# Expert tiles in two phases behind the last attention batch, and the transposed score maxima in another bank

## What is computed

```python
x = x + tanh(g_xattn[0]) * xattn(layernorm(x), ctx, ctx, Wq, bq, Wk, bk, Wv, bv, Wo, bo)
x = x + tanh(g_ffn[0]) * ffn(layernorm(x), norm_scale, w_router, w_up, w_down)

def ffn(x, ...):                       # 8 experts, 352 hidden values, the best 2 of 8 for each token
    xn = rms_norm(x, norm_scale)
    scores = einsum('bsd,ed->bse', xn, w_router)
    _, ids = top_k(scores, 2)
    c = take_along_axis(softmax(scores), ids)
    val, gate = split(einsum('bsd,ehd->bseh', xn, w_up), 2)
    y = einsum('bseh,edh->bsed', val * silu(gate), w_down)
    return sum(take(y, ids) * c) + x
```

## Time and profile before

| what | us |
|---|---|
| median of 3 runs | 489.53 |
| lowest and highest of them | 489.14, 492.61 |
| the profiled execution | 488.46 |
| its span, first to last instruction | 486.7 |
| busy: PE, DVE, ACT, POOL | 395.8, 300.7, 259.8, 249.0 |
| first send, last send of the expert tiles (start) | 308.38, 480.38 |

### The profile page before, as it was taken

One profiled execution on the slowest core, in us unless ns is written; L12 is line 12 of the kernel. 1 busy time (PEld: TensorE's weight loads), 2 busy tenths in 40 slices (PEclk: granted clock), 3 DMA queues, 4 the chain that ended last, 5 costly groups with the idle time before them and its releaser, 6 DMA issues.

```text
span 486.7 us, 13346 instructions
## 1 busy us (share of the span) xinstructions
PE 395.8 (81%) x3788; PEld 269.2 (55%) x3789; DVE 300.7 (62%) x1112; ACT 259.8 (53%) x578; POOL 249.0 (51%) x205
## 2 busy tenths in 40 slices
PE   7578788888979788897987313999999999999960
PEld 3234445464655546455644202777777778777750
DVE  6377678788877887877773430555555555555440
ACT  3232658687676777785757301555455555545520
POOL 4464204136544565635344562456675665667574
PEclk9867899989899998998979555999999999999996
DMA  6331514037377703314011122334353443444230
GB/s 182 105 89 41 143 35 126 22 111 195 87 203 222 185 25 99 92 57 144 26 42 58 55 82 61 65 50 61 52 60 47 57 55 50 55 53 60 21 27 4
DMA packets 57413, 38.99 MB, mean 80 GB/s; under 512 B 8820, under 2 KB 55031, under 8 KB 57367
## 3 DMA queue, kind: packets, MB, share of 16 engines
q1 hardware_dynamic: 42614, 28.24, 22.0%
q0 software_dynamic: 12736, 8.64, 12.8%
q10 hardware_dynamic: 2016, 1.52, 1.2%
HBM read 14.29 MB, written 11.75 MB: 54 GB/s over the span
## 4 chain that ended last, share of the span: by engine, by line
PE 50%; DVE 16%; issue 10%; DMA 9%; ACT 4%; SPq 4%; POOL 3%; POOLq 2%; ACTq 1%; another core or an unknown queue 1%; DVEq 0%
DMA out<-ys,yi 7%; PE bank L1373 6%; PE bank L1351 6%; PE bank L1353 6%; DVE nmx L769 4%; PE bank L1176 4%; PE bank L1363 3%; SPq L237 3%; PE bank L1163 3%; PE bank L1097 2%; PE bank L1193 2%; PE bank L1150 2%; PE bank L1209 2%; ACT pt L542 2%; PE bank L1205 2%
## 5 line engine op out<-in xcount | busy, mean ns | idle before, releaser
L481 POOL DMA_INDIRECT out<-ys,yi x72 | 112.3, 1559 | 74.5 <-issue 37.1
L401 POOL DMA_INDIRECT slots_dram<-xr,slu x64 | 63.8, 997 | 69.3 <-ACT pt L542 47.5
L769 DVE TENSOR_REDUCE nmx<-bank 128x4 f32<-128x512 f32 x128 | 85.7, 676 | 11.9 <-PE bank L1150 11.5
L542 ACT ACTIVATE pt<-bank 128x512 f32<-128x512 f32 x128 | 72.9, 595 | 17.3 <-PE bank L1163 16.5
L1056 DVE TENSOR_TENSOR hh<-sg,bank 128x352 f32<-128x352 f32 x72 | 37.5, 521 | 54.3 <-PE bank L1353 39.3
L1373 PEld LDWEIGHTS bank<-wf_sb,hT 128*128 128x128 f32 (+1 forms) x432 | 56.7, 190 | 23.7 <-issue 19.8
L1373 PE MATMUL bank<-wf_sb,hT 128*128 (+1 forms) x432 | 61.0, 277 | 4.0 <-DVE hT L1066 4.0
L688 ACT ACTIVATE ys<-bank,yc 128x128 f32<-128x128 f32 x72 | 26.4, 367 | 63.7 <-PE bank L1373 33.4
L1351 PE MATMUL bank<-wf_sb,xT 128*128 x144 | 56.0, 471 | 0.0
L1176 PE MATMUL bank<-pt,v 128*9 128x128 f32 x1024 | 50.8, 282 | 6.1 <-ACT pt L542 5.3
L1353 PE MATMUL bank<-wf_sb,xT 128*128 x144 | 55.0, 464 | 0.0
(11 more groups left out here) (163 smaller groups left out, 708.2 us busy)
## 6 DMA issues: line engine op xcount, KB each, us to landing
qs<-parts SPq DMA_DIRECT2D x48, 128.0 KB
ks<-parts SPq DMA_DIRECT2D x42, 128.0 KB
xs<-slots_dram SPq DMA_DIRECT2D x72, 66.0 KB
wf_sb<-in_wup SPq DMA_DIRECT2D x8, 352.0 KB
x_sb<-in_x SPq DMA_DIRECT2D x8, 256.0 KB, 3.3
ctx_sb<-in_ctx_in SPq DMA_DIRECT2D x8, 256.0 KB
out<-x_sb SPq DMA_DIRECT2D x8, 256.0 KB
out<-ys,yi POOLq DMA_INDIRECT x72
```

Of the source, the lines that this page charges most:

```text
L401: nc.gpsimd.indirect_dma_start(out=slots_dram, out_offset=bass.IndirectOffsetOnAxis(ap=slu[:, c % 2, k, kk:kk + 1], axis=0), in_=xr[:, c % ...
L481: nc.gpsimd.indirect_dma_start(out=out.rearrange("b s d -> (b s) d"), out_offset=bass.IndirectOffsetOnAxis(ap=yi[:, r:r + 1], axis=0), in_ ...
L542: nc.scalar.activation(pt[:, 4 * g:4 * g + 4, :], STB[g % 2][:, :].rearrange("p (h s) -> p h s", h=4), ACT.Exp, scale=SCORE_SCALE).then_in ...
L769: nc.vector.tensor_reduce(nmx[:, b % 2, at:at + 4], SB[g % 2][:, :].rearrange("p (h s) -> p h s", h=4), AX.X, ALU.max, negate=True).then_i ...
```

## The change

1. **Two phases.** A first phase of TA = 32 tiles takes only full tiles out of the first NA = 5 chunks. Its table is computed inside the attention loop: counts at b = 26, prefix at b = 29, table at b = 30. The second phase takes the other 40 tiles, again in the order of the experts, from a table made at tiles 14 to 20 of the first phase. The 32 is what is surely there: (2 * 5 * 512 - 8 * 127) // 128, rounded down to a multiple of 8.
2. **No tail of the loop.** The attention loop ends with b = 31. What is left of attention and routing for chunks 6 and 7 is handed out between the tiles of the first phase by `routing(t)` (DVE does the row numbers of chunk 6 at tiles 1 to 3, chunk 7 at 7 to 13, the second table at 15 to 20) on PE, ACT and DVE. POOL does the eight scatters of chunk 6 before sends 4 to 7 and those of chunk 7 before sends 14 to 17, two at a time. SP does the stores of chunks 6 and 7 behind the loads of tiles 7 and 19 and all eight pads behind the load of tile 26. `last_rows` on DVE is gone; ACT makes these rows too. `expert_exp` of chunk 7 now runs at tile 9, after the first silu.
3. **Banks.** The results of `down` have one bank (`Y`, bank 7) in place of two, and `down(t)` waits for `result(t - 1)`. Bank 6 (`TB`) is left for the routing.
4. **Maxima.** `mT_ps` moves from SMALL to the second bank of the scores, SB[1]. The transposition of batch b + 2's maxima, their two parts and their DMAs are done in step b where those of b + 1 were done before: PE transposes behind the last `weighted_values`, DVE splits behind the fourth `maximum`. `scores(b, 1)` gets a wait for `maximum_low(b - 1)`, `transpose_attended(b)` waits for `add_attention(b - 1)` in place of `maximum_low(b + 2)`.
5. **Order on DVE.** `choose_masks` and `choose_sum` come before the third `maximum` of their step, `scales2`, `statistics` and `variance` behind the fourth, `take_positions` and `take_scores` before `add_attention`, `widen` behind it.

The core of the diff (the loops' index of the first body and the code that only changes its place are left out):

```diff
+NA = 5
+TA = (2 * NA * CT - E * 127) // 128 // R * R
+TILE0, TILES = (0, TA), (TA, NT - TA)
+QA = TA // R
-        mT_ps = SMALL[0:NH, 256:384]
+        Y, TB = PR, HB
+        mT_ps = SB[1][0:NH, 0:S]
@@ sync
-                if real(b + 1):
-                    maxima(b + 1)
...
+                if real(b + 2):
+                    maxima(b + 2)
...
+                    if isinstance(q, int):
+                        if t == R - 1:
+                            store(NCH - 2)
+                        if t == 19:
+                            store(NCH - 1)
+                        if t == TA - 6:
+                            pads()
+            sp.wait_ge(d_tab, 1)
+            sp.wait_ge(scattered[0], 16 + 128 * ((NA + 1) // 2))
+            sp.wait_ge(scattered[1], 16 + 128 * (NA // 2))
+            for q in range(QA):
+                body(q)
+            sp.wait_ge(d_tab, 2)
+            sp.wait_ge(padded, 16 * E)
+            sp.wait_ge(scattered[0], 16 + 128 * (NCH // 2))
+            sp.wait_ge(scattered[1], 16 + 128 * (NCH // 2))
@@ gpsimd
-            scatter_rest(NCH - 2, 0)
-            scatter_rest(NCH - 1, 0)
+                    if isinstance(q, int):
+                        if 4 <= t < 4 + CH:
+                            scatter_both(NCH - 2, t - 4)
+                        if 14 <= t < 14 + CH:
+                            scatter_both(NCH - 1, t - 14)
@@ scalar
-            for b in range(B + 2 * CH):
+            for b in range(B):
+            def routing(t):
+                if t == 2:
+                    rows(NCH - 1, (0, 1))
+                if t == 3:
+                    rows(NCH - 1, (2, 3))
+                if t == 5:
+                    rows_transposed(NCH - 1)
+                if t == 7:
+                    base(NCH - 1)
+                if t == 9:
+                    expert_exp(NCH - 1)
@@ vector
+                if u == 0 and there(c - 2):
+                    choose_masks(c - 2)
+                    choose_sum(c - 2)
                 if real(b + 2):
                     maximum(b + 2, 2)
+                if real(b + 2):
+                    maximum(b + 2, 3)
...
+                    maximum_high(b + 2)
+                    maximum_low(b + 2)
...
+                if b == CH * (NA + 1) + 2:
+                    tiles_counted(0)
+                if b == CH * (NA + 2) + 1:
+                    tiles_spread(0)
...
+                if b == CH * (NA + 2) + 1:
+                    tiles_taken(0)
+                if b == CH * (NA + 2) + 2:
+                    tiles_listed(0)
+            def routing(t):
+                c = NCH - 2
+                if t == 1:
+                    scales2(c + 1)
+                    probabilities(c, 0)
+                    place_rows(c)
+                if t == 2:
+                    probabilities(c, 1)
+                    place(c)
+                if t == 3:
+                    probabilities(c, 2)
+                    place_numbers(c)
+                c = NCH - 1
+                if t == 7:
+                    take_scores(c)
+                    choose_values(c)
+                if t == 8:
+                    choose_experts(c)
+                if t == 9:
+                    choose_masks(c)
+                    choose_sum(c)
...
+                if t == 15:
+                    tiles_counted(1)
+                if t == 17:
+                    tiles_spread(1)
+                if t == 18:
+                    tiles_taken(1)
+                if t == 20:
+                    tiles_listed(1)
@@ tensor
+                if g == 1 and b:
+                    pe.wait_ge(d_mT, b)
...
-                if b >= 3:
-                    pe.wait_ge(d_x1, b - 2)
                 nc.tensor.transpose(mT_ps, nmx[:, b % 2, :], ident).then_inc(pe_mT, 1)
...
-                if counts(t - 1):
-                    pe.wait_ge(fa_y, t - 1)
+                if counts(t):
+                    pe.wait_ge(fa_y, t)
...
+            def routing(t):
+                if t == 4:
+                    transpose_rows(NCH - 1)
+                if t == 6:
+                    router(NCH - 1, B)
+                if t == 10:
+                    positions(NCH - 1, B)
+                if t == 14:
+                    count_rows(1, B)
+                if t == 16:
+                    count_tiles(1, B)
+                if t == 19:
+                    list_tiles(1, B)
+                if t == 28:
+                    pe.wait_ge(d_tab, 2)
```

More of the change, by code:

```diff
@@ L409, in scatter_between, with scatter_both @@
                     scatter(c, k, kk)
-            def scatter_rest(c, first):
-                for k in range(first, CH):
-                    for kk in range(2):
-                        scatter(c, k, kk)
+            def scatter_both(c, k):
+                for kk in range(2):
+                    scatter(c, k, kk)
             pool.dma_start(tok_sb[:, :, :], tokrow).then_inc(scattered[1], 16)
@@ L487, in _ @@
                 pool.wait_ge(sent[r], 16)
-            pool.wait_ge(out_sem, 16 * NCH)
+            pool.wait_ge(based[0], 16 * (NCH - 2))
             pool.wait_ge(d_tab, 1)
-            send(0)
-            with pool.Fori(1, NT // R) as q:
+            for q in range(QA):
+                send(q)
+            pool.wait_ge(based[1], 16 * 2)
+            pool.wait_ge(d_tab, 2)
+            with pool.Fori(QA, NT // R) as q:
                 send(q)
@@ L701, in body @@
                     result(q, r)
-            body(0)
-            with act.Fori(1, NT // R - 1) as q:
+            for q in range(QA):
+                body(q)
+            with act.Fori(QA, NT // R - 1) as q:
                 body(q)
@@ L1011, in _ @@
                 if real(b - 1):
+                    add_attention(b - 1)
+                if u == 3 and there(c + 3):
+                    widen(c + 3)
+                if b == CH * (NA + 1) + 2:
+                    tiles_counted(0)
+                if b == CH * (NA + 2) + 1:
+                    tiles_spread(0)
+                if real(b - 1):
                     statistics1(b - 1)
@@ L1082, in body @@
                         hidden_down(*tile_after(q, r, 1))
-            body(0)
-            with dve.Fori(1, NT // R - 1) as q:
+            for q in range(QA):
+                body(q)
+            with dve.Fori(QA, NT // R - 1) as q:
                 body(q)
@@ L1388, in body @@
                 for r in range(R):
+                    if isinstance(q, int):
+                        routing(R * q + r)
                     if r == 4:
@@ L1397, in body @@
                         up(*tile_after(q, r, 3), w[r % 4 + 3])
-            body(0)
-            with pe.Fori(1, NT // R - 1) as q:
+            for q in range(QA):
+                body(q)
+            with pe.Fori(QA, NT // R - 1) as q:
                 body(q)
```

262 lines of the change are left out of this document (153 added, 109 removed).

## The result

The changed kernel takes 499.19 us, the kernel before 488.23 (20 runs of each, side by side): a ratio of 1.0153, 95% interval 1.0113 to 1.0193. Ratios here leave out executions that were slow as a whole, half of the changed kernel's 20 among them, so they are not those of the medians, and where the profiled execution of an experiment was such a one (e5, e7, e14, e15), only the durations and starts of single instructions in it are used. I had forecast 478.7. Its profiled execution is 498.64, with a span of 496.5.

The account below looks back on a forecast made before the run. Sends were taken to bound the tile stage from about tile 7, neither PE nor DVE alone attention. Phases -4.8 and attention -6 on the profiled 488.46 gave 477.7; 1.07 more for the median made 478.7 us, range 468 to 491.

Parts of the forecast that it names:

- part 3: Attention stage: shorter waits -8, fewer half-speed matmuls -2, new PE waits +4; -6 us, between -13 and +5.
- The 6 that stands there beside 7.4: Attention: second amount of waits beside `add_attention`'s 7.4; 40% of both counted as won, 5.4 us.
- Part 1: Handover from attention to tiles: first send at 276.5 (275 to 279), -31.9 us.
- The cover of the table: Steps 26, 29 and 30: other work hides the table's visits to DVE and PE; some 3 us if gone.
- Part 2: Tile stage: more restarts and scatters lengthen the send chain to 199.1 us from 172.0, giving back 27.1.
- the first group: First eight scatters between sends, in the first phase: 6.4 us added to the send chain.
- the formula and its 3.8%: Sends of a run of n tiles: 2.15n + 1.82 if even, 2.15n + 2.1 if odd; trace 3.8% above.
- the second group: Last eight scatters between sends, in the first phase: 7.0 us added to the send chain.
- Rival (d): Second phase's first load waits for pads and scatters, a 10 us hole: 488.7; chance 0.22 together with Rival (a).
- Rival (b): Tile stage: sends land later, 4.3 us per 0.1 us of mean landing, 498 at 0.45; chance 0.11.
- Rival (a): Phases give nothing, attention gains 3: 490.0, median 491, no change; chance 0.22 together with Rival (d).
- my -4.8: Net of the two phases: 31.9 us from the earlier start less 27.1 given back by the send chain.

Follow-up runs that it names:

- e5: The changed kernel with no edit, timed again: 499.59 us, ratio 1.0132 to the kernel before.
- e7: The changed kernel with `rotate_q` moved later, behind `add_attention`: 500.46 us, ratio 1.0203 to the kernel before.
- e14: The changed kernel with `rotate_q` alone moved back in front of the two splits of the maxima: ratio 0.9902 to the kernel before.
- e15: The changed kernel with SP issuing the maxima's DMAs before the second key stack and the expert weights: ratio 0.9921 to the kernel before.
- e12: The kernel before with only the new attention stage (maxima and order, no phases): 499.69 us, ratio 1.0191.
- e8: The kernel before, unchanged: 487.93 us, ratio 1.0013.
- e11: The changed kernel with its attention stage put back as before, two phases and one result bank kept: 488.03 us, ratio 1.0009 to the kernel before.
- e10: The changed kernel with POOL's `rotate_k` moved behind its scatters in the third step of a chunk: 498.18 us, ratio 1.022 to the kernel before.
- e9: The changed kernel with no edit, timed again: 500.52 us, ratio 1.0179 to the kernel before.
- e16: The changed kernel with no edit, on another kind of chip: 472.87 us, ratio 0.9900 to the kernel before.
- e2: The kernel before with only the new attention stage (maxima and order, no phases): 481.15 us, ratio 1.0006.
- e1: The changed kernel with its attention stage put back as before, two phases and one result bank kept: 477.11 us, ratio 0.9938 to the kernel before.
- e4: The changed kernel with SP issuing the maxima's DMAs before the second key stack and the expert weights: ratio 0.9936 to the kernel before.
- e13: The kernel before with only `rotate_q` moved, to behind `add_attention`: 492.47 us, ratio 1.0258.

## Why the prediction was wrong

**The step that failed is part 3, attention, put at -6 us, between -13 and +5.** The attention stage ended 16.9 us later. Of that 12.8 are parts 4 and 5 (e12 against e8), which the -6 was for, and 4.4 the phases (e11 against e8), of which the prediction had named 3. I priced the places where waits vanish and where waits appear on semaphores, and wrote of the new order only that "PE now stands at the end of a step ... No row prices this". I never asked what moving `rotate_q` does to an instruction that has no new wait. In the diff `rotate_q` falls behind the splits, and POOL's column of the timeline has its multiplications directly behind two scatters; that a DVE operation can be held beside POOL was to be read in the trace of before, at 127.59 (1.81 us for 128x4). I had read the waits of L1200, L1238 and L1163 on PE, and not the durations on DVE.

The +16.9 by steps: the three held ones 13.2 (5.29, 3.93, 3.97), of which 9.4 are the holds by the comparison with e10 and most of the rest is the 2.70 us that PE waits for late maxima in the first of them; the step at b = 6 2.2, where PE waits 1.4 us (1.37 at 88.05) for maxima issued late on SP; the last step 2.3; the start-up before b = 1 3.4, which is 1.6 in e9 and 0.2 in e16 and whose cause is open; the others together -4.2.

**What of -6 was right.** The waits do go: 7.4 us for `add_attention` to nothing, and the steps at b = 8 and 12 are 1.4 us shorter each. But e2, the order and the bank alone on kind B with nothing held in its late cases, is 1.0006 [0.9969, 1.0042]: not the 6 us, which would be 0.988. I had said 10 of gain less 4, and without the collision the two came out even within 2 us. That the last heads on kind B come at 255.63 against 255.76 fits this, but is two single executions on two chips. So the -6 was too large even where the collision didn't come. The 6 that stands there beside 7.4 has no row; the earlier trace rows has 4.5 in 4 places for the masks.

**Part 1, the first send.** I put it 11.0 us behind the last heads (the terms 265.5 + 0.7 + 7.5 + 2.6 make 276.3, not the 276.5 that I wrote); it is 11.66 in the changed kernel, 11.27 in e16. The cover of the table ("if their cover is gone they cost some 3 us") is gone: the last step takes 6.68 in place of 4.42, 7.94 in e11; PE's transposition of the heads of batch 30 waits 1.45 for the word row of the table:

```profile
275.98 0.63 PE L1316 MATMUL bank<-con,oT 128*128 128x128 f32 x4 [1.45 <-DVE word L985]
```

**Part 2, the send chain.** I wrote 199.1 us; it is 195.35 (197.29 and 192.36 in other runs). By terms: to send 4, 11.7 forecast and 11.3 measured (305.33 - 294.04); scatters in the first group 6.4, where sends 4 to 9 take 19.5 against 13.3 for a run of five without them by the formula and its 3.8% (sends 18 to 23, with none between them, take 13.2), 6.2; the second group 7.0, where 17.7 against 10.8 by the formula makes 6.9; the second phase to send 61 78.3 forecast, 74.6 measured. The restarts are at the tiles named. So the view that the sends are the bound, and give back most of what the early start gains, held. Rival (d) is out: send 32 follows send 31 by 4.36, a restart, with no hole. Rival (b), later landings, is out as well: the restarts take 3.8 to 4.6 us, where they took 4.1 to 5.3 before. Rival (a), "the phases give nothing", is what e11 measured on kind A (1.0009), while e1 found 0.9938 on kind B: my -4.8 was too hopeful by 2 to 5 us, of which the table in the last step is 2 to 3.

**Rivals.** The one on the slow side was a late landing; the true one was contention between DVE and POOL, and it stood nowhere. On a chip of kind B the result was 0.990, and 478.7 of 489.53 is 0.978: the right sign and less than half the size.

The table loads of the exponential cost nothing to be seen: 1.28 us each, and send 9, in front of which they lie, is a restart of 4.22 us anyway.

## What to carry to other kernels

Before moving an instruction on VectorE, look at what GpSimd runs at the new time, and at the durations of both: an instruction whose mean is far above that of its like (1.81 us for 128x4) marks a place where the two engines contend. Where they must meet, let the one on the critical path start first; here a hold of up to 2.9 us on VectorE made PE's step 2 to 4 us longer, while the other order cost GpSimd 1.15 us on an engine with slack. A narrow order of starts that rests on a third engine being in time isn't safe: here PE's signals came a microsecond late on some chips. And measure a change that shifts such an order on more than one chip: it can be 1% faster on one and 1.5% slower on another.

## What the runs showed of the hardware

- A VectorE multiplication of 128x512 f32 (0.67 us) that starts beside a GpSimd scatter with two multiplications directly behind it takes up to 3.57 us (e12); it ends 0.56 after the last of them (117.26 to 120.78, `kb` to 120.22). It is not let in between GpSimd's two multiplications. Beside a scatter with no multiplication directly behind it, it isn't held (0.67 in e10).
- By the starts in the trace the first of two such VectorE multiplications is held where it starts up to 0.51 us before the first of GpSimd's (e12); at 0.57 and 0.67 before (e4) both go on in 0.67, and GpSimd's takes 1.83 and 1.74 in place of 1.28. With 0.71 before (e13, 174.69 and 175.40) the first goes on and the second is held, 3.15. With no scatter directly in front, 0.41 before is not held (0.68 at 83.45 in the kernel before), but the second is, 1.76.
- The other way round, a GpSimd scatter that starts with two such VectorE instructions takes 2.12 in place of 0.97 (e16).
- A TENSOR_SCALAR of 128x4 with one SBUF input was held too (1.81 in place of 0.16), and in another run, at 0.37 behind the scatter in place of 0.36, not.
- Chips differ: between 40 and 262 us, on kind A 35 to 56 of PE's signals come more than 0.5 us behind the modelled end of their matmuls in each profile, on kind B none or one. What waits for them starts late: the cast in front of `rotate_q` 0.31 or 0.32 us behind PE's transposition on kind B, and 1.07, 1.90 and 1.03 in three of the four late cases on kind A. Why is open.
- Behind idle time PE's matmuls can take twice as long: 2.08 in place of 1.02 in the changed kernel behind waits of 2.70 and 1.19 us, with a granted clock of 0.50 from 121 to 127 us.
